# Ternary FFN: biases summed in the matrix products, silu read from its bank, value and product in one pass

## The chip, the cores and the metric

The kernel runs on one core of a Trainium2 chip. The metric is the device time of one execution in microseconds (us), the median of several runs. It is one program of 2.2 ms: four layers, each with a cross attention and a feed-forward network (FFN). The change touches the last FFN alone, which takes the last 130 us.

## What is computed

The activations x are 16 x 128 tokens of 256 features. The last step is `x = x + ffn(layernorm(x))`, with a ternary FFN of 1024 hidden features:

```python
def bit_linear(x, w, b):
    gamma_x = jnp.clip(jnp.max(jnp.abs(x), axis=-1, keepdims=True), 1e-05, None)
    scale_x = 127.0 / gamma_x
    x_dq = jnp.clip(jnp.round(x * scale_x), -128.0, 127.0) / scale_x
    gamma_w = jnp.clip(jnp.mean(jnp.abs(w)), 1e-05, None)
    w_dq = jnp.clip(jnp.round(w / gamma_w), -1.0, 1.0) * gamma_w
    return jnp.einsum('bsd,hd->bsh', x_dq, w_dq) + b
gate = jax.nn.silu(bit_linear(x, gate_w, gate_b))
val = bit_linear(x, val_w, val_b)
return bit_linear(gate * val, out_w, out_b)
```

The kernel multiplies whole numbers held in bf16 (rounded rows by weights of -1, 0 and 1). The sum then has to be multiplied by the row's step (`x_step`, the largest absolute value over 127) and by the weights' mean, and the bias added.

## The kernel before, in words

The 2048 tokens are 16 tiles of 128 rows (`B`), in four groups of four (`GROUP`). `k` is a tile's place in its group. Each engine has its own instruction list, written out in order in `ternary_ffn` (L3369); semaphores (`Signal`) tie the lists together, and `behind(engine, signal, n)` waits for the n-th event, if there is one. Nothing is planned by a program: the order is that of the loops.

TensorE (L3427 to L3469): `up(n, ...)` multiplies tile n by the gate weights into two banks of 512 columns (`gates`), and again by the value weights into two more (`vals`), each bank as two products of 128 rows deep, bf16, 512 columns. For every n its queue holds up(n+1) for the gates, up(n+1) for the values, for k = 2 `turn_rows` (the next group's rounded rows turned), then `turn_product(n)` (eight turns of 128x128, bf16) and `go_down(n)` (eight products of 256 columns into one bank `down`).

VectorE (L3517 to L3581): `halves` reads a bank, multiplies it by the row's scale and adds the bias, for half a tile at a time: gates to `pre`, values to `val` (L3531). `measure(n)` multiplies `val` by silu of `pre` (`prod`, L3547), takes the largest absolute value (L3549), and makes the step and its inverse (L3551, L3552). `finish(n)` adds the downward product to x (L3560). In between stand, for the next group, `norm.scales` and `spread_scales` at k = 0 and `norm.round` at k = 1.

ScalarE (L3471 to L3515): `silu(n)` (L3477, halves), `round_product(n)` (L3481 scales and lifts `prod`, L3484 rounds it to bf16) and `move(n)` (L3489 copies the turned product out of its bank). In iteration n the order is move(n-1), the normalizing of four rows (L2047, at k = 0), their lifting (L2070, at k = 1) or the copy of the turned rows `move_rows` (L3493, at k = 2), round_product(n), silu(n+1).

GpSimd adds the output bias to x (L3425) and takes the root for the norm. SP's queue loads two biases at the start of the stage and stores each tile of the output.

The banks are freed as follows: a gates half once L3531 has read it into `pre`, a values half once L3531 has read it into `val`; `up` waits for that with `behind(pe, read, 2 * (n - 1) + h)`:

```python
for n in range(B):
    if n + 1 < B:
        up(n + 1, gates, w.g, pre_made, gated)
        up(n + 1, vals, w.v, val_made, valued)
    if n % GROUP == 2 and n // GROUP < LASTG:
        turn_rows(n // GROUP + 1)
    turn_product(n)
    go_down(n)
```

The helper `project` (L296) of the first attention, the windowed attention and the mixture-of-experts lines L1861 and L1871 are not touched; the prediction takes durations from them. In `project` two products with f32 operands of 512 columns are issued:

```python
for c in range(HC):
    last = pe.matmul(proj[m % 2][:, :], lhs[:, c, :], weight[:, c, :], start=(c == 0), stop=(c == HC - 1))
```

L1861 copies a bank of 256 columns, L1871 does so with a scale per partition (`moe_share`); L783 is an activation of 512 columns read from a bank.

Of the kernel before, what the change touches and what calls it, by code (L numbers as in the profile page):

```python
# [14 lines left out]
P = 128  # L15
# [911 lines left out]
GROUP = 4  # L927
# [2441 lines left out]
def ternary_ffn(nc, mem, out, stored, norm):  # L3369
# [6 lines left out]
    with ctx:  # L3376
# [11 lines left out]
        pre, gate, val, prod, shifted = (sb(x, [P, F]) for x in ("pre", "gate", "val", "prod", "shifted"))  # L3388
# [18 lines left out]
        pre_made, val_made, silued, multiplied = signal("pre"), signal("val"), signal("silued"), signal("multiplied")  # L3407
# [8 lines left out]
        with nc.Block() as block:  # L3416
# [11 lines left out]
            def _(pe):  # L3428
                def up(n, out_banks, weight, read, done):
                    pe.wait_ge(rows_moved.sem, rows_moved.at(n // GROUP))  # L3430
                    for h in range(2):
                        behind(pe, read, 2 * (n - 1) + h)
                        for c in range(HC):
                            last = pe.matmul(out_banks[h][:, :], mem.xnt16[:, c, n * P:(n + 1) * P], weight[:, c, h * HALF:(h + 1) * HALF], start=(c == 0), stop=(c == HC - 1))  # L3434
                        last.then_inc(done.sem, 1)
# [24 lines left out]
                up(0, gates, w.g, pre_made, gated)  # L3460
                up(0, vals, w.v, val_made, valued)
                for n in range(B):
                    if n + 1 < B:
                        up(n + 1, gates, w.g, pre_made, gated)
                        up(n + 1, vals, w.v, val_made, valued)
# [6 lines left out]
            def _(act):  # L3472
                def silu(n):
                    behind(act, multiplied, n - 1)
                    for h in range(2):
                        act.wait_ge(pre_made.sem, pre_made.at(2 * n + h))
                        act.activation(gate[:, h * HALF:(h + 1) * HALF], pre[:, h * HALF:(h + 1) * HALF], ACT.Silu).then_inc(silued.sem, 1)  # L3477
# [40 lines left out]
            def _(dve):  # L3518
# [6 lines left out]
                def halves(n, target, banks, scale, bias, made, done, read):  # L3525
                    dve.wait_ge(spread.sem, spread.at(2 * (n // GROUP) + 1))
                    for h in range(2):
                        cols = slice(h * HALF, (h + 1) * HALF)
                        dve.wait_ge(made.sem, made.at(2 * n + h))
                        behind(dve, *read(n, h))  # L3530
                        dve.scalar_tensor_tensor(target[:, cols], banks[h][:, :], scale[:, n:n + 1], bias[:, cols], ALU.mult, ALU.add).then_inc(done.sem, 1)  # L3531

                def before_silu(n):
# [390 lines left out]
```

## Time and profile before

| | us |
|---|---|
| median of 3 runs | 2207.52 |
| lowest, highest | 2202.86, 2207.97 |
| the profiled execution | 2204.45 |
| its span, first to last instruction | 2202.7 |
| TensorE busy in the span | 1928.3 (88%) |
| VectorE busy | 1348.5 (61%) |
| ScalarE busy | 1065.7 (48%) |
| GpSimd busy | 717.3 (33%) |

Of the span's 40 slices of 55 us the last two and a half hold the ternary FFN. In the page's rows of engines PE is TensorE's matrix products, PEld its weight loads, DVE VectorE, ACT ScalarE, POOL GpSimd. PEclk is the granted TensorE clock, 1.00 being 2.4 GHz and 0.50 being 1.2 GHz. A row of the timeline has its start and its length in us; where several instructions are merged, "x4" is their number, and the length runs from the first one's start to the last one's end. The bracket at its end is the idle time of the engine ahead of it, with what ended it.

### The profile page before, as it was taken

The page shows a single profiled execution, that of the slowest core. Times are in us where ns is not written, and L with a number is a line of the kernel's source. Part 1 is how long each engine was busy: PE and PEld are TensorE (multiplying, and loading weights), DVE is VectorE, ACT ScalarE, POOL GpSimd, SP SyncE. Part 2 cuts the span into 40 slices and gives each one's busy share as a digit, 9 for nine tenths or more (in the row PEclk, how much of TensorE's full clock was granted, in tenths as well). Part 3 has the DMA queues.
Part 4 walks back from the last instruction along what each step waited for, and adds up shares of the span by engine and source line. Part 5 has one row for each costly group of instructions (what it writes and reads, how often), then busy time and mean ns, then how long its engine had stood idle before and what let it go on. Part 6 is the DMA issues. An engine that isn't in the chain of part 4 may idle for free. (4 is left out here: it accounts for less than half of the span.)

```text
span 2202.7 us, 42217 instructions
## 1 busy us (share of the span) xinstructions
PE 1928.3 (88%) x11925; PEld 1297.9 (59%) x11926; DVE 1348.5 (61%) x3440; ACT 1065.7 (48%) x2793; POOL 717.3 (33%) x691
## 2 busy tenths in 40 slices
PE   7999999998999899979899989979967889888655
PEld 4666666665656566645676667635534557776433
DVE  6556556565777344446443434469969447777687
ACT  5545444553333222112344434357769437677575
POOL 3323333331000004443455556523200026666310
PEclk9999999999999889869999999989979989999787
DMA  9980000000000001143677777600010111111100
GB/s 310 279 223 0 0 0 0 0 1 1 0 0 0 1 1 61 61 162 104 146 160 173 163 164 127 125 1 2 1 60 1 65 36 34 30 40 31 31 17 22
DMA packets 145576, 145.11 MB, mean 66 GB/s; under 512 B 49376, under 2 KB 133568, under 8 KB 145344
## 3 DMA queue, kind: packets, MB, share of 16 engines
q1 hardware_dynamic: 122432, 113.81, 18.2%
q0 software_dynamic: 23040, 30.01, 7.9%
q8 instruction: 53, 0.87, 0.2%
q14 instruction: 51, 0.42, 0.1%
HBM read 137.12 MB, written 66.44 MB: 92 GB/s over the span
## 5 line engine op out<-in xcount | busy, mean ns | idle before, releaser
L1686 POOL DMA_INDIRECT expert_sums<-moe_rows_in,moe_to x128 | 197.9, 1546 | 158.0 <-DMA expert_sums<-moe_rows_in,moe_to 85.9
L1759 PE MATMUL moe_gate<-moe_places,moe_xt 128*128 x512 | 175.5, 465 | 3.1 <-issue 1.9
L1949 DVE COPY moe_ht_e<-moe_turned 128x256 f32<-128x256 f32 x128 | 54.3, 424 | 194.1 <-PE moe_turned L1767 194.1
L619 ACT ACTIVATE ga_prob<-ga_score,ga_neg_max 128x128 f32<-128x128 f32 x256 | 99.5, 390 | 145.7 <-DVE ga_neg_max L493 145.7
L240 POOL TENSOR_TENSOR ga_q_inv<-ga_q_sum,half 128x4 f32<-128x4 f32 x64 | 64.4, 1007 | 304.3 <-DVE ga_q_sum L476 304.3
L3017 POOL TENSOR_TENSOR wa_low<-wa_low,wa_top 128x512 f32<-128x512 f32 x128 | 133.0, 1039 | 89.8 <-DVE wa_top L3221 89.0
L2039 POOL TENSOR_TENSOR ln_rstd<-ln_var,half 128x4 f32<-128x4 f32 (+1 forms) x16 | 21.8, 1361 | 351.9 <-DVE ln_var L2035 351.8
L1153 POOL DMA_INDIRECT slot_x<-early x96 | 93.9, 979 | 112.0 <-DVE early L1144 73.3
L375 PE MATMUL ga_summed<-ga_wo,ga_out_t 128*128 128x256 f32 x512 | 122.5, 383 | 0.7 <-ACT ga_out_t L627 0.7
L375 PEld LDWEIGHTS ga_summed<-ga_wo,ga_out_t 128*128 128x128 f32 x512 | 98.1, 192 | 40.6 <-issue 29.2
L3218 DVE SCALAR_TENSOR_TENSOR wa_low<-wa_score,early 128x512 f32<-128x512 f32 x128 | 87.7, 685 | 55.0 <-PE wa_score L3057 52.5
L299 PE MATMUL ga_proj<-early,ga_xt 128*128 128x512 f32 x252 | 118.6, 593 | 0.0
L1759 PEld LDWEIGHTS moe_gate<-moe_places,moe_xt 128*128 128x128 f32 x512 | 90.7, 189 | 46.6 <-issue 11.5
L489 DVE SCALAR_TENSOR_TENSOR ga_score<-ga_scored,ga_q_inv,ga_mask 128x128 f32<-128x128 f32 x256 | 72.2, 344 | 68.1 <-PE ga_scored L347 51.4
L3155 ACT ACTIVATE wa_probs<-wa_low 128x512 f32<-128x512 f32 x128 | 80.6, 630 | 66.9 <-POOL wa_low L3017 65.9
L3221 DVE TENSOR_REDUCE wa_top<-wa_low 128x4 f32<-128x512 f32 x128 | 87.8, 686 | 4.4
L3057 PE MATMUL wa_score<-wa_keys,wa_qd 32*128 32x128 f32 x1024 | 78.4, 293 | 13.3 <-POOL wa_qd L3011 7.2
L3066 PE MATMUL wa_turned<-ident,wa_probs 128*128 128x128 f32 x512 | 86.4, 294 | 3.6 <-ACT wa_probs L3155 3.0
L1866 ACT ACTIVATE moe_act_e<-moe_gate 128x176 f32<-128x176 f32 x128 | 40.6, 317 | 99.5 <-PE moe_gate L1759 99.5
L506 DVE COPY ga_prob_t<-ga_turned_p 128x256 f32<-128x256 f32 x128 | 48.2, 418 | 65.2 <-PE ga_turned_p L355 65.0
L3057 PEld LDWEIGHTS wa_score<-wa_keys,wa_qd 32*128 32x128 f32 x1024 | 66.1, 195 | 27.5 <-issue 25.3
L3161 ACT ACTIVATE wa_pt<-wa_turned 128x512 f32<-128x512 f32 x128 | 74.4, 581 | 13.1 <-PE wa_turned L3066 13.0
(482 smaller groups left out, 4952.0 us busy)
## 6 DMA issues: line engine op xcount, KB each, us to landing
moe_places<-in_L_ffn_packed SPq DMA_DIRECT2D x128, 608.0 KB
slot_x<-zeros SPq DMA_DIRECT2D x24, 1076.0 KB, 16.1
moe_rows_in<-slot_x SPq DMA_DIRECT2D x128, 134.5 KB, 2.7
wa_v<-v_ctx SPq DMA_DIRECT2D x16, 180.0 KB, 3.1
early<-in_L_xattn_Wq SPq DMA_DIRECT2D x5, 512.0 KB, 7.8
x<-in_x SPq DMA_DIRECT2D x4, 512.0 KB, 9.2
ga_wo<-in_L_xattn_Wo SPq DMA_DIRECT2D x1, 2048.0 KB, 14.0
expert_sums<-zeros SPq DMA_DIRECT2D x2, 1024.0 KB, 8.2
```

Source lines behind the costliest of these rows:

```text
L299: last = pe.matmul(proj[m % 2][:, :], lhs[:, c, :], weight[:, c, :], start=(c == 0), stop=(c == HC - 1))
L375: last = pe.matmul(summed[:, 0:H], out_t[:, h, :], w.wo[:, h, :], start=(h == 0), stop=(h == NH - 1))
L619: last = act.activation(prob[:, n % 2, part], score[:, n % 2, part], ACT.Exp, bias=neg_max[:, n % 2, h:h + 1], accum_out=total[:, n % 2, h ...
L1153: pool.indirect_dma_start(out=self.mem.slot_x, out_offset=bass.IndirectOffsetOnAxis(ap=self.slot_to[:, t, k:k + 1], axis=0), in_=self.mem. ...
L1686: pool.indirect_dma_start(out=mem.sums[j % SUMS], out_offset=bass.IndirectOffsetOnAxis(ap=to[:, j:j + 1], axis=0), in_=y[:, j, :], in_offs ...
L1759: last = pe.matmul(both[j % 2][:, 0:2 * FE], xt[:, j % 2, c, :], packed[:, place, c * 2 * FE:(c + 1) * 2 * FE].rearrange("p a n -> p (a n) ...
L3017: pool.tensor_tensor(unit, unit, top[:, k % LOWS, :].unsqueeze(2).to_broadcast([P, QUAD, P]), ALU.subtract).then_inc(lowered.sem, 1)
L3057: last = pe.matmul(score[BANK[r]][:, x * P:(x + 1) * P], qd[rows, j % 2, QUAD * u + x, :], keys[rows, j % 2, QUAD * u + x, :], start=True, ...
L3066: last = pe.transpose(turned[k % 2][:, x * P:(x + 1) * P], probs[:, k % 2, x, :], mem.ident[:, :])
L3155: act.activation(probs[:, k % 2, :, :], low[:, k % LOWS, :, :], ACT.Exp).then_inc(exped.sem, 1)
L3218: dve.scalar_tensor_tensor(unit.rearrange("p x n -> p (x n)"), score[BANK[k % QUAD]][:, :], WD ** -0.5, w.table[:, k, :, :].rearrange("p x ...
L3221: dve.tensor_reduce(top[:, k % LOWS, :], unit, AX.X, ALU.max).then_inc(topped.sem, 1)
```

## The change

The bias is summed by TensorE. The bank holds whole numbers that are later multiplied by step and mean, so the bias must go in divided by both: once at the start `bias_over_mean` divides the two bias tiles (128x1024, f32, in place) by the weights' means, and `spread_inverse(n)` makes, for each tile, a 128x128 f32 diagonal of the rows' inverse steps (two buffers). `up` gets a third product per half: diagonal by bias, 512 columns, both operands f32, in the same accumulation. The gates' bank is then read by ScalarE's silu, with the scale as its operand, and `pre` goes; the values' bank is read by the product pass, half by half, and `val` goes. So a gates half is free after silu, a values half after the product.

```diff
--- before.py
+++ after.py
@@ -3385,7 +3385,8 @@
 
         w = mem.tf
         scale_g, scale_v = sb("scale_g", [P, B]), sb("scale_v", [P, B])
-        pre, gate, val, prod, shifted = (sb(x, [P, F]) for x in ("pre", "gate", "val", "prod", "shifted"))
+        gate, prod, shifted = (sb(x, [P, F]) for x in ("gate", "prod", "shifted"))
+        diagonal, per_mean = sb("diagonal", [P, 2, P]), sb("per_mean", [P, 2])
         rounded = sb("rounded", [P, F], BF16)
         ht = sb("ht", [P, FC, P], BF16)
         up_by, down_by = sb("up_by", [P, 1]), sb("down_by", [P, 1])
@@ -3404,7 +3405,8 @@
         spread = signal("spread")
         biased = signal("biased")
         gated, valued = signal("gated"), signal("valued")
-        pre_made, val_made, silued, multiplied = signal("pre"), signal("val"), signal("silued"), signal("multiplied")
+        diagonals, per_means, biases = signal("diagonals"), signal("per_means"), signal("biases")
+        silued, multiplied = signal("silued"), signal("multiplied")
         chain, per_made = signal("chain"), signal("per")
         lifted, rounded_s = signal("lifted"), signal("rounded")
         turn, moved, downed, added = signal("turn"), signal("moved"), signal("downed"), signal("added")
@@ -3426,13 +3428,16 @@
 
             @block.tensor
             def _(pe):
-                def up(n, out_banks, weight, read, done):
+                def up(n, out_banks, weight, bias, j, read, done):
                     pe.wait_ge(rows_moved.sem, rows_moved.at(n // GROUP))
                     for h in range(2):
                         behind(pe, read, 2 * (n - 1) + h)
                         for c in range(HC):
-                            last = pe.matmul(out_banks[h][:, :], mem.xnt16[:, c, n * P:(n + 1) * P], weight[:, c, h * HALF:(h + 1) * HALF], start=(c == 0), stop=(c == HC - 1))
-                        last.then_inc(done.sem, 1)
+                            pe.matmul(out_banks[h][:, :], mem.xnt16[:, c, n * P:(n + 1) * P], weight[:, c, h * HALF:(h + 1) * HALF], start=(c == 0), stop=False)
+                        if h == 0:
+                            pe.wait_ge(diagonals.sem, diagonals.at(n))
+                            pe.wait_ge(biases.sem, biases.at(j))
+                        pe.matmul(out_banks[h][:, :], diagonal[:, n % 2, :], bias[:, h * HALF:(h + 1) * HALF], start=False, stop=True).then_inc(done.sem, 1)
 
                 def turn_rows(g):
                     pe.wait_ge(norm.rounded.sem, norm.rounded.at(g * GROUP + GROUP - 1))
@@ -3457,12 +3462,12 @@
                     last.then_inc(downed.sem, 1)
 
                 turn_rows(0)
-                up(0, gates, w.g, pre_made, gated)
-                up(0, vals, w.v, val_made, valued)
+                up(0, gates, w.g, w.bg, 0, silued, gated)
+                up(0, vals, w.v, w.bv, 1, multiplied, valued)
                 for n in range(B):
                     if n + 1 < B:
-                        up(n + 1, gates, w.g, pre_made, gated)
-                        up(n + 1, vals, w.v, val_made, valued)
+                        up(n + 1, gates, w.g, w.bg, 0, silued, gated)
+                        up(n + 1, vals, w.v, w.bv, 1, multiplied, valued)
                     if n % GROUP == 2 and n // GROUP < LASTG:
                         turn_rows(n // GROUP + 1)
                     turn_product(n)
@@ -3471,10 +3476,11 @@
             @block.scalar
             def _(act):
                 def silu(n):
-                    behind(act, multiplied, n - 1)
+                    act.wait_ge(spread.sem, spread.at(2 * (n // GROUP)))
                     for h in range(2):
-                        act.wait_ge(pre_made.sem, pre_made.at(2 * n + h))
-                        act.activation(gate[:, h * HALF:(h + 1) * HALF], pre[:, h * HALF:(h + 1) * HALF], ACT.Silu).then_inc(silued.sem, 1)
+                        behind(act, multiplied, 2 * (n - 1) + h)
+                        act.wait_ge(gated.sem, gated.at(2 * n + h))
+                        act.activation(gate[:, h * HALF:(h + 1) * HALF], gates[h][:, :], ACT.Silu, scale=scale_g[:, n:n + 1]).then_inc(silued.sem, 1)
 
                 def round_product(n):
                     act.wait_ge(per_made.sem, per_made.at(n))
@@ -3522,17 +3528,15 @@
                     for scale, mean_of in ((scale_g, w.mean_g), (scale_v, w.mean_v)):
                         dve.tensor_scalar(scale[:, cols], mem.x_step[:, cols], mean_of[:, 0:1], None, ALU.mult).then_inc(spread.sem, 1)
 
-                def halves(n, target, banks, scale, bias, made, done, read):
-                    dve.wait_ge(spread.sem, spread.at(2 * (n // GROUP) + 1))
-                    for h in range(2):
-                        cols = slice(h * HALF, (h + 1) * HALF)
-                        dve.wait_ge(made.sem, made.at(2 * n + h))
-                        behind(dve, *read(n, h))
-                        dve.scalar_tensor_tensor(target[:, cols], banks[h][:, :], scale[:, n:n + 1], bias[:, cols], ALU.mult, ALU.add).then_inc(done.sem, 1)
-
-                def before_silu(n):
-                    halves(n, pre, gates, scale_g, w.bg, gated, pre_made, lambda n, h: (silued, 2 * (n - 1) + h))
-                    halves(n, val, vals, scale_v, w.bv, valued, val_made, lambda n, h: (multiplied, n - 1))
+                def spread_inverse(n):
+                    if n % GROUP == 0:
+                        dve.wait_ge(norm.scaled.sem, norm.scaled.at(n // GROUP))
+                    behind(dve, valued, 2 * (n - 2) + 1)
+                    dve.tensor_scalar(diagonal[:, n % 2, :], mem.ident[:, :], norm.scale[:, n:n + 1], None, ALU.mult).then_inc(diagonals.sem, 1)
+
+                def bias_over_mean(j, bias):
+                    dve.wait_ge(per_means.sem, per_means.at(j))
+                    dve.tensor_scalar(bias[:, :], bias[:, :], per_mean[:, j:j + 1], None, ALU.mult).then_inc(biases.sem, 1)
 
                 def measure(n):
                     j = slice(n % 2, n % 2 + 1)
@@ -3541,11 +3545,14 @@
                         ins.then_inc(chain.sem, 1)
                         dve.wait_ge(chain.sem, chain.at(2 * n + k))
 
-                    dve.wait_ge(silued.sem, silued.at(2 * n + 1))
-                    dve.wait_ge(val_made.sem, val_made.at(2 * n + 1))
+                    dve.wait_ge(spread.sem, spread.at(2 * (n // GROUP) + 1))
                     behind(dve, lifted, n - 1)
-                    dve.tensor_tensor(prod[:, :], val[:, :], gate[:, :], ALU.mult).then_inc(multiplied.sem, 1)
-                    dve.wait_ge(multiplied.sem, multiplied.at(n))
+                    for h in range(2):
+                        dve.wait_ge(valued.sem, valued.at(2 * n + h))
+                        dve.wait_ge(silued.sem, silued.at(2 * n + h))
+                        dve.scalar_tensor_tensor(prod[:, h * HALF:(h + 1) * HALF], vals[h][:, :], scale_v[:, n:n + 1], gate[:, h * HALF:(h + 1) * HALF],
+                                                 ALU.mult, ALU.mult).then_inc(multiplied.sem, 1)
+                    dve.wait_ge(multiplied.sem, multiplied.at(2 * n + 1))
                     step(0, dve.tensor_reduce(far[:, j], prod[:, :], AX.X, ALU.max, apply_absolute_value=True))
                     behind(dve, added, n - 2)
                     step(1, dve.tensor_scalar(size[:, j], far[:, j], 1e-5, 1.0 / 127.0, ALU.max, ALU.mult))
@@ -3560,12 +3567,18 @@
                     dve.scalar_tensor_tensor(row, down[:, 0:H], scale_o[:, n % 2:n % 2 + 1], row, ALU.mult, ALU.add).then_inc(added.sem, 1)
 
                 spread_scales(0)
+                spread_inverse(0)
+                for j, mean_of in enumerate((w.mean_g, w.mean_v)):
+                    dve.reciprocal(per_mean[:, j:j + 1], mean_of[:, 0:1]).then_inc(per_means.sem, 1)
+                bias_over_mean(0, w.bg)
                 norm.variance(dve, LASTG * GROUP, B)
                 norm.shifts(dve, 1, LASTG * GROUP, B)
                 dve.wait_ge(mem.tf_loaded.sem, 16 * 3)
-                before_silu(0)
+                bias_over_mean(1, w.bv)
                 for n in range(B):
                     g, k = divmod(n, GROUP)
+                    if n + 1 < B:
+                        spread_inverse(n + 1)
                     measure(n)
                     if k == 0 and g < LASTG:
                         norm.scales(dve, g + 1)
@@ -3574,8 +3587,6 @@
                         if g >= 2:
                             dve.wait_ge(turned_rows.sem, turned_rows.at(g - 1))
                         norm.round(dve, g + 1)
-                    if n + 1 < B:
-                        before_silu(n + 1)
                     if n >= 1:
                         finish(n - 1)
                 finish(B - 1)
```

## Rows read from the trace of the kernel before

**Rows 1.** Windows of the ternary FFN: us, busy us (count) by engine, PEclk, DMA share, GB/s.

```profile
2105.00:2135.00 30.00, 18.46 (x106) 10.10 (x104) 26.22 (x50) 22.59 (x29) 2.77 (x4) 0.78 0.05 18
```

**Rows 2.** Chain that ended last, near its end: start us, us, what.

```profile
2184.43 1.23 DVE tf_far L3549
...
2186.07 1.25 ACT tf_shifted L3481
...
2187.41 0.04 ACT tf_rounded L3484
...
2188.46 1.14 ACT tf_gate L3477 x2
...
2189.63 1.24 DVE tf_prod L3547
```

**Rows 3.** Timeline of the ternary FFN: start us, us, engine, line, what [idle before].

```profile
2095.37 1.05 PE L3456 MATMUL tf_down<-tf_o,tf_ht 128*128 128x256 bf16 x8 [1.33 <-ACT tf_ht L3489]
...
2096.25 1.03 PE L3434 MATMUL tf_gates<-tf_g,tf_xnt 128*128 128x512 bf16 x4
...
2097.59 1.40 DVE L3531 SCALAR_TENSOR_TENSOR tf_pre<-tf_gates,tf_scale_g,early 128x512 f32<-128x512 f32 x2
...
2098.62 1.02 ACT L3493 ACTIVATE tf_xnt<-tf_turned_in 128x1024 bf16<-128x1024 bf16 x1 [3.31 <-PE tf_turned_in L3442]
...
2102.07 0.62 PE L3449 MATMUL tf_turned<-ident,tf_rounded 128*128 128x128 bf16 x8 [3.48 <-ACT tf_rounded L3484]
...
2102.96 1.00 ACT L3489 ACTIVATE tf_ht<-tf_turned 128x1024 bf16<-128x1024 bf16 x1
...
2104.02 1.89 PE L3456 MATMUL tf_down<-tf_o,tf_ht 128*128 128x256 bf16 x8 [1.32 <-ACT tf_ht L3489]
...
2105.70 1.56 PE L3434 MATMUL tf_gates<-tf_g,tf_xnt 128*128 128x512 bf16 x4
...
2110.32 2.07 ACT L2047 ACTIVATE tf_rows_of<-x,ln_shift,ln_rstd 128x256 f32<-128x256 f32 x4
...
2110.47 1.05 PE L3456 MATMUL tf_down<-tf_o,tf_ht 128*128 128x256 bf16 x8 [1.33 <-ACT tf_ht L3489]
...
2125.19 1.05 PE L3456 MATMUL tf_down<-tf_o,tf_ht 128*128 128x256 bf16 x8 [1.12 <-ACT tf_ht L3489]
...
2134.05 1.89 PE L3456 MATMUL tf_down<-tf_o,tf_ht 128*128 128x256 bf16 x8 [1.12 <-ACT tf_ht L3489]
...
2140.29 1.05 PE L3456 MATMUL tf_down<-tf_o,tf_ht 128*128 128x256 bf16 x8 [1.33 <-ACT tf_ht L3489]
```

**Rows 4.** Groups by line and shape: busy us, mean ns of one, idle before.

```profile
L1178 DVE TENSOR_SCALAR early<-ident,early 128x128 f32<-128x128 f32 x1 | 0.3, 289 | 0.0
...
L783 ACT ACTIVATE sf_act_g<-sf_gate 128x512 f32<-128x512 f32 x32 | 19.1, 596 | 93.6 <-PE sf_up L743 93.6
...
L1861 ACT ACTIVATE moe_xt<-moe_up 128x256 f32<-128x256 f32 x128 | 49.2, 384 | 48.6 <-PE moe_up L1748 38.0
...
L1871 ACT ACTIVATE moe_rows_in<-moe_pairs,moe_share 128x256 f32<-128x256 f32 x64 | 30.3, 473 | 31.3 <-PE moe_pairs L1774 31.3
```

**Rows 5.** Timeline of TensorE in the first attention, and windows of two attentions.

```profile
51.91 1.88 PE L299 MATMUL ga_proj<-early,ga_xt 128*128 128x512 f32 x4
...
44.00:64.00 20.00, 19.66 (x106) 14.78 (x105) 13.97 (x42) 13.91 (x59) 7.44 (x9) 1.00 0.79 217
...
1840.00:1860.00 20.00, 17.29 (x299) 13.72 (x298) 16.09 (x31) 14.06 (x26) 12.37 (x13) 1.00 0.15 30
```

**Rows 6.** Timeline around the start of the ternary FFN.

```profile
2057.39 1.14 DVE L2065 TENSOR_SCALAR early<-early,ln_scale 128x256 f32<-128x256 f32 x4
...
2075.47 1.89 PE L3434 MATMUL tf_gates<-tf_g,tf_xnt 128*128 128x512 bf16 x4 [1.18 <-ACT tf_xnt L3493]
...
2080.02 1.03 PE L3434 MATMUL tf_vals<-tf_v,tf_xnt 128*128 128x512 bf16 x4
```

**Rows 7.** Timeline at the end of the span.

```profile
2199.23 0.48 DVE L3560 SCALAR_TENSOR_TENSOR x<-tf_down,tf_scale_o,x 128x256 f32<-128x256 f32 x1 [6.24 <-PE tf_down L3456]
```

## The prediction, made before the change was run

> **What bounds the kernel now.** I read the windows first, then the chain of waits, then the timeline of one tile, then the costs by shape. The windows say where the stage stands [rows 1]: in the ternary FFN VectorE is busy 26.2 of 30 us, ScalarE 22.6, TensorE 18.5 at a mean granted clock of 0.78. So VectorE looks like the bound, and the change unloads it. The chain corrects this [rows 2]: near the end one loop closes in about 6.45 us: product 1.24, maximum 1.23, step and inverse 0.41 up to the start of the scaling, scaling 1.25 and 0.09 of waits, rounding 1.05 until silu can follow it, silu 1.14, and some 0.06 of waits. It crosses VectorE and ScalarE, and TensorE is not in it. In the timeline the reader should look for what is queued on TensorE: down(n-1), gates and values of n+1, turn of the product n, in that fixed order. One group of four tiles takes 29.8 us (down at 2110.47 to down at 2140.29), and in each group ScalarE stands 3.31 us in front of the row copy L3493, because TensorE turns the rows only behind the up products [rows 3].
>
> A measurement of this kernel can tell about 0.3% (7 us) from no change.
>
> **Part 1, removed from VectorE.** Four L3531 passes (two in 1.40 us, so 2.80) and one L3547 (1.24) go; two passes of L3531's kind, bank times scalar times SBUF tile, come back at 1.40; the new diagonal is 128x128 in f32, 0.29 us by L1178's row, less beside others. Net 4.04 - 1.69 = 2.3 us per tile less VectorE [rows 2 to 4]. That is 37 us over 16 tiles, but only a stretch that ends on VectorE gives any of it back.
>
> **Part 2, silu from the bank.** From a bank 128x512 takes 0.60 us (L783), and a scale per partition costs 0.473 - 0.384 = 0.09 more (L1871 against L1861): 0.69. The pair, 1.14 now, goes to about 1.28 (0.69 and 0.60 behind it): +0.15 on ScalarE [rows 2, 4]. The product can now start on half 0 when silu of half 0 is done. The old loop becomes: silu 0.69, two product passes with the second from 1.37 to 2.11, maximum until 3.37, step and inverse until 3.75, scaling and rounding until the next silu at 6.15. So without TensorE the loop would be 6.15 instead of 6.45.
>
> **Part 3, the bias in the accumulator.** Four matrix products of 128x512 per tile are added, with both operands f32. What they cost stands elsewhere in this trace: the project helper issues two f32 products of 128x512, and the trace has four records in 1.88 us at clock 1.00, that is four times 0.427 and 0.17 of fill [rows 5]. So one f32 product is two records, 0.853 us; the bf16 one takes 0.213 (four in 1.03, with the same fill) [rows 6]. Per tile: 4 x 0.853 = 3.41 us more on TensorE at full clock, 6.8 at half clock. Bounds: not under 0.213 each (bf16's row, if the form did not matter), not over 1.71 (half clock throughout). I take 0.853, from the same shape and type.
>
> TensorE's queue is in order and closes its own loop: from down to the up products 0.88 (2095.37 to 2096.25); up 4 x 0.213 x 2 = 1.71, with the biases 5.12; turn 0.62; semaphore 0.05; ScalarE's copy L3489 1.00; semaphore 0.06; next down. **7.75 us** per tile. That is above 6.15 and above today's 6.45, so TensorE becomes the bound. New waits, and who queues there: the gates of n+1 wait for silu(n), the values for product(n); counted from the end of up(n), product(n) ends 0.75 later (the second half's pass behind its values), maximum, step, inverse, scaling and rounding take the way to 4.9, silu(n+1) ends at 6.2 and product(n+1) at 8.5, while the gates of n+2 come up at 10.35 (7.75 + 0.62 + 1.11 + 0.88) and their values at 12.9. Both waits are met 4 us early, so they cost nothing; with that cover gone, TensorE and everything in its queue would stand for what silu or product is late. The waits on the diagonals and biases stand ahead of the first bias product of each half; VectorE makes the diagonal of n+1 ahead of measure(n), one tile early: nothing. No DMA is added or moved, SP's queue is as before. GpSimd's biases of x and its root stay; only the first root comes later (below).
>
> The normalizing rows on ScalarE (2.07 us, twice in a group) [rows 3] fall into its idle time: its own work there is 1.28 + 1.00 + 2.07 + 2.39 = 6.7, under 7.75. So tiles k = 0, 1 and 3 of a group take 7.75; today k = 0 and 1 take 14.72 together (2110.47 to 2125.19) and k = 3 takes 6.24 (2134.05 to 2140.29) [rows 3].
>
> **The tile k = 2** is the expensive one. Its way is down, up products, turn of the rows, row copy L3493, scaling and rounding, silu, copy of the turned product, down: 8.65 us in the first group (2095.37 to 2104.02), 8.86 in the second (2125.19 to 2134.05) [rows 3]. All of the up products lie on it, so it becomes 12.2 to 12.4 with 3.41 and 0.15 added; I take 12.3.
>
> **The clock.** In the trace TensorE drops to half after this very gap: idle 3.48 us, turn, idle again, then down in 1.89 instead of 1.05 and the gates behind it in 1.56 [rows 3]. The changed kernel keeps a gap of about 3.4 us there. Down and most of the gates, 3 us of work, run at half clock in that row, so 1.5 us are lost; the drop may last some gates longer, 2.1 at most by my estimate if all of the gates are in it. It now lies on the path, as up does. I take 1.7 per group. Elsewhere TensorE has 6.65 us of work in 7.75, and the windowed attention, busy 17.29 of 20 us, runs at 1.00 [rows 5]. The Trainium skill, page "TensorE: Matmul & The Clock Gate", section "What's actually happening", says that activity releases the throttle and idleness brings it back; read so, denser work might keep the full clock through this gap too, and then the terms for it fall away. By that rule the trace agrees that gaps precede the drops; it does not show TensorE this busy beside such a gap. This is rival A.
>
> **Start.** VectorE does the bias pass of 1024 columns ahead of variance. Its price: 0.29 for 128 columns, and four passes of 256 in 1.14 us give up to 0.27 per 256; so 0.5 to 1.2, I take 1.0 [rows 4, 6]. The gates start at 2075.47 as now, the bias is ready near 2075.1; root and shift end near 2077.2, the bias of the values near 2078.2, all ahead of TensorE. It is at half clock at first (four products in 1.89) and back at full before 2080.02 (1.03); I take 2079.6. So gates are done at 2080.1, values at 2082.65, product(0) at 2083.45 [rows 6]. Maximum, step and inverse take it to 2085.05, scaling and rounding to 2087.4, silu(1) to 2088.65, the copy to 2089.65: down(0) comes at about 2089.7.
>
> **Sum.** Down(0) 2089.7; +7.75; +12.3; +7.75 + 1.7 gives down(3) at 2119.2. Two groups of 7.75 x 3 + 12.3 + 1.7 = 37.25: down(11) at 2193.7. Down(13) two loops later, 2209.2. Product(15) ends 6.0 + 0.75 behind it: 2215.95. From the end of product(15) (2189.63 + 1.24) to the end of the span today 2202.7 - 2190.87 = 11.83 us pass, the last addition at 2199.23 in them, and that tail is untouched [rows 2, 7]. End 2227.8: **+25 us** on the span of 2202.7. The profiled execution's own time of 2204.45 becomes 2229.5; it lies 3.1 us under the median of the three runs, 2207.52, so the median should come near 2232 by the one reference and 2229.5 by the other. I predict 2231, between them.
>
> **Rivals.**
> A. As above but the clock holds at full behind the row copy: 3 x 1.7 less, +20, 2226. For it: TensorE does more between the gaps. Against: the 3.48 us gap shown is followed by half clock, and so is its like in the next group, down again 1.89 at 2134.05 [rows 3].
> B. Half clock reaches further, for the small gap of 1.1 us in every tile: some 2 us more in each of half a dozen tiles, +37, 2243. The trace has a gap of 1.33 us in front of a down at full clock (1.05) [rows 3], so I hold it unlikely.
> C. The other side, faster: the accumulation hides the bias at bf16's price. TensorE's loop is then 0.88 + 2.56 + 0.62 + 1.11 = 5.2 and the loop of 6.15 decides, the point being a bias product under about 0.45 us (7.75 - 4 x 0.4 = 6.15). Plain tiles gain 0.3; with the pressure off VectorE the tiles with normalizing gain up to 1; k = 2 still gets longer by about 1.0. Together up to 1 per group and 1 to 4 over the rest: 2195 to 2204, under 0.3% for the most part, the low end only if the clock holds too. Against it stand the two records per f32 product [rows 5].
> D. VectorE is the bound after all, as its busy share says: 16 x 2.3 = 37 us less, 2170. Against: in rows 2 it waits for ScalarE's silu, and TensorE's 7.75 is above either loop.
> E. The edit does not do what it says, the f32 pair is skipped or merged: same as C at its upper end, no change.
>
> **Chances.** Forecast 0.66, A 0.16, B 0.10, C 0.05 (0.03 of it faster), D 0.01, E 0.02. Slower by over 0.3% is 0.92, within 0.04, faster 0.04. The range takes in A and goes 7 us under it, for the start (1 us), for a k = 2 tile at its lower value and for the 5 us by which the runs differ; above it goes to the near part of B: 2219 to 2241. It leaves out C, D, E and half of B, 0.13, and tails.
>
> **What the new profile would show.** Right: four bias products per tile as eight records of 0.427 us spacing; TensorE busy over 85% in the stage; plain tiles 7.75 apart, the k = 2 tile near 12.3; VectorE idle in front of the product with the values named as releaser; down in 1.89 behind the row copy. Wrong: bias records with bf16's spacing, ScalarE's silu instead of TensorE's values in front of the product, or plain tiles near 6.2, each of which would put the result at or under today's time.

## The result and the profile after

The changed kernel takes 2231.91 us (median of four runs, 2226.65 to 2245.17) against 2207.74 for the kernel before (four runs, 2202.86 to 2213.69): a ratio of 1.0118, with a 95% interval of 1.0082 to 1.0155. It is slower by 24 us by the medians and by 26 by the ratio; 2231 was predicted. That agreement has to be read with a margin: the profiled execution has a span of 2235.2 us against 2202.7, which is 32.5 more, and only part of that belongs to the change. Its first gate product starts 6.7 us later (2082.16 against 2075.47), behind stages that are the same code in both kernels. The part from there to the end of the span, "the stage" below, is what the change touches: 2202.7 - 2075.47 = 127.23 us before, 2235.2 - 2082.16 = 153.04 after, 25.8 us more. The prediction's own times (2227.8 - 2075.47) make it 152.3.

The windows of the changed kernel, with the columns of [rows 1]:

```profile
2105.00:2135.00 30.00, 23.17 (x108) 12.40 (x107) 13.55 (x32) 17.79 (x23) 2.79 (x4) 0.89 0.04 13
2165.00:2200.00 35.00, 28.17 (x127) 14.57 (x125) 15.90 (x37) 20.64 (x26) 1.94 (x3) 0.90 0.05 16
```

VectorE's 26.2 of 30 us [rows 1] are down to 13.6, so the unloading worked as built. Over the whole stage its work falls less, from 103.2 to 70.6 us, 2.03 per tile; the rest of the fall in the window is that the tiles are longer. TensorE is up from 18.5 to 23.2 and its clock from 0.78 to 0.89, and the stage is longer all the same. The chain of waits says why. Its columns are start us, us, what. The four pieces of f32 products (L3440) take 3.4 of each 7.8 us:

```profile
2096.48 1.05 PE tf_down L3461 x8
2097.96 0.86 PE tf_gates L3440 x2
2099.25 0.86 PE tf_gates L3440 x2
2100.54 0.86 PE tf_vals L3440 x2
2101.83 0.86 PE tf_vals L3440 x2
2103.17 1.03 ACT tf_ht L3495
2104.25 1.05 PE tf_down L3461 x8
```

Nothing of VectorE is in this stretch, and of ScalarE only the copy L3495. This is TensorE's own loop: 2096.48 to 2104.25 is 7.77 us. The chain of [rows 2], product, maximum, scaling, rounding, silu, is gone from it.

Groups by line and shape in the stage, after (busy us, mean ns, idle before and what ended it):

```profile
L3440 PE MATMUL tf_gates<-early,tf_diagonal 128*128 128x512 f32 x64 | 35.9, 645 | 0.0
L3440 PE MATMUL tf_vals<-tf_bv,tf_diagonal 128*128 128x512 f32 x64 | 32.7, 592 | 0.0
L3553 DVE SCALAR_TENSOR_TENSOR tf_prod<-tf_vals,tf_scale_v,tf_gate 128x512 f32<-128x512 f32 x32 | 23.6, 750 | 65.7 <-PE tf_vals L3440 38.0 <-ACT tf_gate L3483 27.7
```

The price is in the counts: 64 f32 products are issued, one for each of two biases, two halves and 16 tiles. Each of the two groups has 64 records for 32 products, so two per product. VectorE's product pass stood 65.7 us idle, 38.0 of them for TensorE's values.

The timeline of TensorE over the k = 2 tile, after, and then the row copy on ScalarE:

```profile
2108.15 1.02 PE L3440 MATMUL tf_vals<-tf_bv,tf_diagonal 128*128 128x512 f32 x2
...
2110.30 0.61 PE L3447 MATMUL tf_turned_in<-ident,tf_out_of 128*128 128x128 bf16 x8
2114.39 1.03 PE L3454 MATMUL tf_turned<-ident,tf_rounded 128*128 128x128 bf16 x8 [3.48 <-ACT tf_rounded L3490]
2116.54 1.89 PE L3461 MATMUL tf_down<-tf_o,tf_ht 128*128 128x256 bf16 x8 [1.12 <-ACT tf_ht L3495]
2118.22 1.06 PE L3436 MATMUL tf_gates<-tf_g,tf_xnt 128*128 128x512 bf16 x2
2119.08 1.65 PE L3440 MATMUL tf_gates<-early,tf_diagonal 128*128 128x512 f32 x2
...
2126.16 1.05 PE L3461 MATMUL tf_down<-tf_o,tf_ht 128*128 128x256 bf16 x8 [1.12 <-ACT tf_ht L3495]
```

```profile
2110.94 1.02 ACT L3499 ACTIVATE tf_xnt<-tf_turned_in 128x1024 bf16<-128x1024 bf16 x1 [6.75 <-PE tf_turned_in L3447]
```

This answers [rows 3]. ScalarE stands 6.75 us in front of the row copy instead of 3.31; TensorE's gap of 3.48 us is there again; behind it the turns (1.03) and down (1.89) run at half clock, then the gates, and full clock is back within the first f32 pair (1.65, where a pair takes 1.02 at full clock). The tile k = 2 takes 2116.54 - 2104.25 = 12.29 us, the one behind it 9.62, the next 7.77.

### The profile page after: what moved, and what is told of

It is laid out like the page before. It is cut to its first block and busy times, and to the rows that moved or that the text cites. A ratio compares the mean times of both kernels' runs of the same rounds, so it can differ in the third digit from the quotient of the medians.

```text
span 2235.2 us, 42466 instructions
## 1 busy us (share of the span) xinstructions
PE 1980.5 (89%) x12053; PEld 1325.0 (59%) x12054; DVE 1316.8 (59%) x3412; ACT 1069.5 (48%) x2793; POOL 717.1 (32%) x691
## 5 line engine op out<-in xcount | busy, mean ns | idle before, releaser
L1759 PEld LDWEIGHTS moe_gate<-moe_places,moe_xt 128*128 128x128 f32 x512 | 91.4, 191 | 47.1 <-issue 12.3
L3057 PEld LDWEIGHTS wa_score<-wa_keys,wa_qd 32*128 32x128 f32 x1024 | 67.3, 199 | 27.7 <-issue 25.5
## 6 DMA issues: line engine op xcount, KB each, us to landing
ga_wo<-in_L_xattn_Wo SPq DMA_DIRECT2D x1, 2048.0 KB, 14.2
```

Of the source, the lines that this page charges most:

```text
L1759: last = pe.matmul(both[j % 2][:, 0:2 * FE], xt[:, j % 2, c, :], packed[:, place, c * 2 * FE:(c + 1) * 2 * FE].rearrange("p a n -> p (a n) ...
L3057: last = pe.matmul(score[BANK[r]][:, x * P:(x + 1) * P], qd[rows, j % 2, QUAD * u + x, :], keys[rows, j % 2, QUAD * u + x, :], start=True, ...
```

## The experiments

The ratio is that of each kernel against the kernel before on the same chip; e1 to e4 ran on one chip, e5 to e8 on a second, e9 and e10 on a third, so whole times of different groups are not compared. In these traces the first gate product starts anywhere from 2075 to 2109 us, up to 34 us apart and up to 16.5 on one chip, in code that no kernel here changes, so the stage is the sharper measure. It comes from one trace per kernel; how far it repeats is known only from e3 and e10, the same kernel on two chips: 117.3 and 117.0. Where the trace lacks the record of the first gate product (the idle time ahead of the first one shown is 1.58 us instead of 1.18), 0.4 us are added; those are marked with a star.

| kernel | bias products | rows turned | stage, us | ratio (95% interval) |
|---|---|---|---|---|
| before | none, biases on VectorE | behind up | 127.2 | 1 |
| the change | f32 | behind up | 153.0 | 1.0118 (1.0082 to 1.0155) |
| e1_fp16 | fp16 | behind up | 127.1 | 1.001 (0.9991 to 1.0028) |
| e2_early | f32 | ahead of up | 135.7 | 1.0056 (1.0036 to 1.0075) |
| e3_fp16_early | fp16 | ahead of up | 117.3 | 0.9948 (0.9927 to 0.9969) |
| e4_before_early | none, on VectorE | ahead of up | 121.7 | 0.9993 (0.9972 to 1.0015) |
| e5_double | f32, twice | behind up | 208.1* | not known, one run |
| e6_warm | f32, one gap filled | behind up | 150.4* | 1.0112 (1.0082 to 1.0143) |
| e7_half | f32, gates only | behind up | 130.6* | 1.0034 (1.0005 to 1.0062) |
| e8_nobias | left out | behind up | 120.5* | 0.9974 (0.9952 to 0.9995) |
| e9_warm2 | f32, both gaps filled | behind up | 147.6* | 1.008 (1.0045 to 1.0114) |
| e10_fp16_early2 | as e3 | ahead of up | 117.0* | 0.9927 (0.9897 to 0.9958) |

### Is it the price of the f32 products?

e1_fp16 writes the diagonal and the divided biases as 16-bit floats and changes nothing else:

```diff
-        diagonal, per_mean = sb("diagonal", [P, 2, P]), sb("per_mean", [P, 2])
+        diagonal, per_mean = sb("diagonal", [P, 2, P], F16), sb("per_mean", [P, 2])
+        bias_g, bias_v = sb("bias_g", [P, F], F16), sb("bias_v", [P, F], F16)
...
-                up(0, gates, w.g, w.bg, 0, silued, gated)
+                up(0, gates, w.g, bias_g, 0, silued, gated)
...
-                    dve.tensor_scalar(bias[:, :], bias[:, :], per_mean[:, j:j + 1], None, ALU.mult).then_inc(biases.sem, 1)
+                    dve.tensor_scalar(out[:, :], bias[:, :], per_mean[:, j:j + 1], None, ALU.mult).then_inc(biases.sem, 1)
```

> The diagonal and the two bias tiles are written as 16-bit floats (fp16), so each bias product is of the bf16 kind; everything else is the changed kernel. Theory P (the price of the f32 products, 0.853 us each, makes TensorE the bound): one record per bias product at 0.21 us spacing, TensorE's loop falls from 7.77 to about 5.2 us, the loop through silu, product and rounding (6.15) decides in plain tiles, the k = 2 tile near 9.6 to 9.8; the stage from its first gate product to the end of the span falls from 153 to about 122 to 127 us, the whole to 2195 to 2208. Rival S (it is the structure: silu and the product now hold the banks and the chain): the stage stays above 145 us.

Measured: the stage falls from 153.0 to 127.1, the upper edge of what was expected, and the kernel is back at the time of the one before. Same rows, same banks, same waits: so the structure (rival S) is not what costs. An fp16 bias product (f16 in the rows) is one record, and the next product starts 0.22 us behind it. Timeline of TensorE, e1:

```profile
2116.76 1.05 PE L3463 MATMUL tf_down<-tf_o,tf_ht 128*128 128x256 bf16 x8 [1.12 <-ACT tf_ht L3497]
...
2118.07 0.38 PE L3442 MATMUL tf_gates<-tf_bias_g,tf_diagonal 128*128 128x512 f16 x1
2118.29 0.59 PE L3438 MATMUL tf_gates<-tf_g,tf_xnt 128*128 128x512 bf16 x2
...
2126.39 1.89 PE L3463 MATMUL tf_down<-tf_o,tf_ht 128*128 128x256 bf16 x8 [1.44 <-ACT tf_ht L3497]
...
2134.15 1.05 PE L3463 MATMUL tf_down<-tf_o,tf_ht 128*128 128x256 bf16 x8 [1.12 <-ACT tf_ht L3497]
...
2138.48 0.62 PE L3456 MATMUL tf_turned<-ident,tf_rounded 128*128 128x128 bf16 x8 [0.69 <-ACT tf_rounded L3492]
2140.54 1.05 PE L3463 MATMUL tf_down<-tf_o,tf_ht 128*128 128x256 bf16 x8 [1.44 <-ACT tf_ht L3497]
```

The k = 2 tile (2116.76 to 2126.39) takes 9.63 instead of 12.29, a tile with normalizing rows (2134.15 to 2140.54) 6.39, where 6.15 was expected. What keeps the stage from the lower edge is the clock: tile 1 takes 8.09 and the first two k = 3 tiles 7.76 and 8.03, with most of their up products at half clock. Now TensorE waits 0.69 us for ScalarE's rounding in front of the turns, which it did not in the f32 version.

e5_double goes the other way and issues the f32 bias product twice, so that the biases count double:

```diff
+                        pe.matmul(out_banks[h][:, :], diagonal[:, n % 2, :], bias[:, h * HALF:(h + 1) * HALF], start=False, stop=False)
                         pe.matmul(out_banks[h][:, :], diagonal[:, n % 2, :], bias[:, h * HALF:(h + 1) * HALF], start=False, stop=True).then_inc(done.sem, 1)
```

> The f32 bias product is issued twice in each half (the bias counts double in the output). Theory P: every tile is on TensorE's loop, so each tile gets 4 x 0.853 = 3.41 us more: plain tiles 11.18, the k = 2 tile 15.7, the stage 153 + 16 x 3.41 = 207.6 us. Rival S (the structure limits): TensorE has slack and the stage grows by under 30 us.

```profile
2111.03 1.05 PE L3462 MATMUL tf_down<-tf_o,tf_ht 128*128 128x256 bf16 x8 [1.12 <-ACT tf_ht L3496]
...
2122.24 1.05 PE L3462 MATMUL tf_down<-tf_o,tf_ht 128*128 128x256 bf16 x8 [1.12 <-ACT tf_ht L3496]
...
2137.96 1.89 PE L3462 MATMUL tf_down<-tf_o,tf_ht 128*128 128x256 bf16 x8 [1.12 <-ACT tf_ht L3496]
```

In this timeline of TensorE a plain tile takes 11.21 us, 3.44 more than 7.77, and the k = 2 tile 15.72, 3.43 more than 12.29. The stage grows by 55.0 us, 16 times 3.44. Every 0.853 us added to TensorE is paid in full: in the changed kernel it has no slack.

e7_half leaves the bias of the values out of the computation, e8_nobias both biases. The edit of e7, whose bf16 products then end the accumulation where no bias product follows:

```diff
-                        pe.matmul(out_banks[h][:, :], diagonal[:, n % 2, :], bias[:, h * HALF:(h + 1) * HALF], start=False, stop=True).then_inc(done.sem, 1)
+                        if j == 0:
...
+                            last = pe.matmul(out_banks[h][:, :], diagonal[:, n % 2, :], bias[:, h * HALF:(h + 1) * HALF], start=False, stop=True)
+                        last.then_inc(done.sem, 1)
```

> The f32 bias product is issued for the gates alone; the values' bias is left out of the computation. Theory P: TensorE's loop is 7.77 - 1.71 = 6.06, just under the loop through silu and product as the fp16 version showed it (6.27 in the last group), so plain tiles in the last group take 6.3 and those with normalizing rows 6.4; k = 2 takes 12.29 - 1.71 = 10.6, k = 3 some 8; a group 31.4, the stage about 132 us. If the cost per product were all that counts, without a second loop, plain tiles would be 6.06.

```profile
2192.86 1.05 PE L3463 MATMUL tf_down<-tf_o,tf_ht 128*128 128x256 bf16 x8 [1.12 <-ACT tf_ht L3497]
...
2198.98 1.05 PE L3463 MATMUL tf_down<-tf_o,tf_ht 128*128 128x256 bf16 x8 [1.18 <-ACT tf_ht L3497]
...
2205.25 1.05 PE L3463 MATMUL tf_down<-tf_o,tf_ht 128*128 128x256 bf16 x8 [1.33 <-ACT tf_ht L3497]
```

The last group of e7 runs at 6.12 and 6.27 us per tile (2192.86, 2198.98, 2205.25). In the groups before it, tiles with normalizing rows take 6.40 and k = 2 10.48 to 10.57. From down(1) to down(5) are 31.7, and the stage is 130.6 where about 132 was expected. TensorE's own loop would be 6.06. The 6.40 lies clear of it, so there the loop through ScalarE and VectorE decides. In the last group the two are too close to tell: its tiles take 6.05, 6.12, 6.27 and 6.13.

> No bias product at all (both biases are left out); the diagonals are still made. Theory P: nothing is gained over the fp16 version in plain tiles (6.3 to 6.4, set by ScalarE and VectorE), and 0.85 us in each k = 2 tile (8.8): the stage about 124.5 us against its 127.1. Rival S: as in the fp16 version, over 145.

Timeline of TensorE, e8:

```profile
2177.61 1.05 PE L3458 MATMUL tf_down<-tf_o,tf_ht 128*128 128x256 bf16 x8 [1.37 <-ACT tf_ht L3492]
...
2183.89 1.05 PE L3458 MATMUL tf_down<-tf_o,tf_ht 128*128 128x256 bf16 x8 [1.45 <-ACT tf_ht L3492]
```

Measured: plain tiles 6.27 and 6.28, those with normalizing rows mostly 6.39 as in e1, k = 2 8.77 and 8.85, the stage 120.5 where 124.5 was expected. The rule for plain tiles held, and 6.27 is the loop without TensorE. The miss of 4 us lies mostly in tiles that run at half clock: there TensorE's loop is the longer one again, and a bias product left out is worth 0.43 us instead of 0.21. Tile 1 takes 6.39 in e8 and 8.09 in e1, the first two k = 3 tiles 7.18 and 6.19 against 7.76 and 8.03. With e1, e5, e7 and e8 the curve is known for tiles at full clock: flat up to some 6.2 us of TensorE loop, and one to one above.

### Is it the row turns behind the up products?

e2_early moves one statement in TensorE's list:

```diff
                 for n in range(B):
+                    if n % GROUP == 2 and n // GROUP < LASTG:
+                        turn_rows(n // GROUP + 1)
                     if n + 1 < B:
                         up(n + 1, gates, w.g, w.bg, 0, silued, gated)
                         up(n + 1, vals, w.v, w.bv, 1, multiplied, valued)
-                    if n % GROUP == 2 and n // GROUP < LASTG:
-                        turn_rows(n // GROUP + 1)
                     turn_product(n)
```

> The changed kernel with f32 products, but at k = 2 TensorE turns the next group's rows ahead of the up products instead of behind them. Theory P: the k = 2 tile no longer has all up products ahead of the row copy; it falls from 12.29 to about 8.2 us (7.77 and the turns), the gap of 3.48 us goes and the half clock behind it too, so the next tile falls from 9.62 to about 7.8; together 3 x 5.9 = 18 us less than the changed kernel, about 2214, and the stage 135. Rival: the row copy is not what holds the tile, then under 5 us are gained.

```profile
2119.24 1.05 PE L3461 MATMUL tf_down<-tf_o,tf_ht 128*128 128x256 bf16 x8 [1.12 <-ACT tf_ht L3495]
2120.12 0.61 PE L3447 MATMUL tf_turned_in<-ident,tf_out_of 128*128 128x128 bf16 x8
...
2127.45 1.05 PE L3461 MATMUL tf_down<-tf_o,tf_ht 128*128 128x256 bf16 x8 [1.12 <-ACT tf_ht L3495]
```

The k = 2 tile is 2127.45 - 2119.24 = 8.21 us, no gap is left but the 1.12 us in front of down, and down runs at 1.05. The stage falls by 17.3 us: the f32 products are dearest where the whole of up stands ahead of something that ScalarE waits for.

e4_before_early is the same move in the kernel before.

> The kernel before, with only the rows turned ahead of the up products at k = 2. ScalarE's wait of 3.31 us in front of the row copy falls to about 1.3, so some 2 us per group are gained, 6 in all: about 2201, the stage 121. If VectorE's 26 of 30 us are the true bound of that kernel, it gains nothing.

```profile
2113.88 1.02 ACT L3493 ACTIVATE tf_xnt<-tf_turned_in 128x1024 bf16<-128x1024 bf16 x1 [1.58 <-PE tf_turned_in L3442]
```

ScalarE's wait for the row turns falls from 3.31 to 1.58 us, the stage from 127.2 to 121.7 as expected. The times of the whole kernel show less, 0.9993 with an interval that holds 1: 5.5 us are a quarter of a per cent, which these runs cannot tell. With e2 this says what the order has to do with the change: the order alone is worth 5.5 us without bias products. With the rows turned early in both kernels, the f32 biases cost 14.0 us (121.7 to 135.7) instead of 25.8. So 11.8 of the 25.8 us hang on the order.

e3_fp16_early puts fp16 and the early row turns together.

> Both of the former: fp16 bias products and the rows turned early. Theory P: ScalarE's own work decides at k = 0 and 1 (6.75), k = 2 near 7.3, k = 3 near 6.2, a group 27 instead of 29.8 us before the change; the stage about 115 to 118 us instead of 127, the whole about 2196, 0.5% faster than before. Rival S: not faster than before.

```profile
2128.07 1.05 PE L3463 MATMUL tf_down<-tf_o,tf_ht 128*128 128x256 bf16 x8 [1.12 <-ACT tf_ht L3497]
...
2135.12 1.89 PE L3463 MATMUL tf_down<-tf_o,tf_ht 128*128 128x256 bf16 x8 [1.45 <-ACT tf_ht L3497]
...
2146.14 0.62 PE L3456 MATMUL tf_turned<-ident,tf_rounded 128*128 128x128 bf16 x8 [0.69 <-ACT tf_rounded L3492]
2148.21 1.70 PE L3463 MATMUL tf_down<-tf_o,tf_ht 128*128 128x256 bf16 x8 [1.45 <-ACT tf_ht L3497]
...
2155.09 1.05 PE L3463 MATMUL tf_down<-tf_o,tf_ht 128*128 128x256 bf16 x8 [1.12 <-ACT tf_ht L3497]
...
2201.86 1.05 PE L3463 MATMUL tf_down<-tf_o,tf_ht 128*128 128x256 bf16 x8 [1.45 <-ACT tf_ht L3497]
...
2208.13 1.05 PE L3463 MATMUL tf_down<-tf_o,tf_ht 128*128 128x256 bf16 x8 [1.45 <-ACT tf_ht L3497]
```

A group (2128.07 to 2155.09) takes 27.0 us, 27 expected; the k = 2 tile 7.05, plain tiles of the last group 6.27. The tiles k = 0 and 1 take 6.40 and 6.88, not 6.75 each. The stage is 117.3 us, 10 less than before the change and 36 less than after it. Of the 10 us, 5.5 are the order's (e4) and 4.4 belong to the change with fp16 biases (121.7 to 117.3). The ratio of 0.9948 is clear of 1 and of the change's 1.0118. It was run again:

> The version with fp16 bias products and the rows turned early once more, on whatever chip comes: the earlier stages differ by up to 20 us from run to run, so its gain of 0.5% over the kernel before is to be seen a second time. By the stages (117.3 against 127.2 us) it should be 10 us, a ratio of 0.995.

Measured: 0.9927 (0.9897 to 0.9958), the stage 117.0. This version beats both kernels. Its biases carry the rounding of fp16 twice, in the inverse step and in the bias over the mean.

### Is half clock behind the gap the gap's doing?

e6_warm gives TensorE something to do in the 3.48 us:

```diff
+        idle = bank("idle")
...
                         turn_rows(n // GROUP + 1)
+                        for i in range(14):
+                            pe.matmul(idle[:, :], mem.xnt16[:, 0, n * P:(n + 1) * P], w.g[:, 0, 0:HALF], start=True, stop=True)
```

> The changed kernel with 14 idle bf16 products of 512 columns (3.0 us at full clock, into a bank of their own that nobody reads) behind the turns of the rows at k = 2, where TensorE stands 3.48 us. Clock theory: the gap is filled, so the down behind it takes 1.05 instead of 1.89 us and its tile 7.8 instead of 9.6; three times 1.85 = 5.5 us less, the stage 147.5. Rival: the fall has another cause; down stays at 1.89 and the stage at 153.

```profile
2107.13 2.97 PE L3475 MATMUL tf_idle<-tf_g,tf_xnt 128*128 128x512 bf16 x13
2110.56 0.62 PE L3455 MATMUL tf_turned<-ident,tf_rounded 128*128 128x128 bf16 x8 [0.46 <-ACT tf_rounded L3493]
2112.63 1.53 PE L3462 MATMUL tf_down<-tf_o,tf_ht 128*128 128x256 bf16 x8 [1.45 <-ACT tf_ht L3498]
```

A half miss. The turns run at full clock now, but the clock falls inside the down behind them: 1.53 us here, 1.19 in the second group, 1.05 in the third, where no fall comes. The tile behind takes 9.45, about as long as 9.62, in the first group and 7.77 in the third. The stage falls to 150.4. Two gaps are left, 0.46 and 1.45 us, so e9_warm2 fills the second as well:

```diff
                     turn_product(n)
+                    if n % GROUP == 2 and n // GROUP < LASTG:
+                        for i in range(5):
+                            pe.matmul(idle[:, :], mem.xnt16[:, 0, n * P:(n + 1) * P], w.g[:, 0, 0:HALF], start=True, stop=True)
                     go_down(n)
```

> The changed kernel with both gaps of the k = 2 tile filled: 14 idle bf16 products behind the turns of the rows, and 5 more (1.07 us) between the turns of the product and down. With the first gap alone filled, the clock still fell in two of three groups, late, inside down or right behind it. Clock theory: with both filled it stays at full in all three, every down but the last takes 1.05, every k = 3 tile 7.8, the stage 147.5 us. Rival: what is left of the fall does not come from the gaps; one or more of the three downs is still slow and the stage at 150.

```profile
2137.58 0.62 PE L3455 MATMUL tf_turned<-ident,tf_rounded 128*128 128x128 bf16 x8 [0.46 <-ACT tf_rounded L3496]
2138.03 1.24 PE L3479 MATMUL tf_idle<-tf_g,tf_xnt 128*128 128x512 bf16 x5
2139.64 1.05 PE L3462 MATMUL tf_down<-tf_o,tf_ht 128*128 128x256 bf16 x8 [0.37 <-ACT tf_ht L3501]
```

Every down but the last takes 1.05 us, in all three groups; each k = 3 tile takes 7.77; the stage is 147.6. The fall belongs to the gaps, both of them, and costs 5.4 us in this kernel. The products whose result nobody reads lengthen nothing, as TensorE stood still there: the k = 2 tile takes 12.20.

## Why the prediction was right, point by point

- **f32 products.** 0.853 us each and two records per product were taken from the projections of the first attention [rows 5]. The trace after has 64 records for 32 products, and e5 measures 3.44 per tile for four, 0.86 each. Rival C, bf16's price, is excluded.
- **TensorE's loop.** 7.75 predicted, 7.77 measured in every tile with k = 0 or 1 and in the last group up to down(14). The move of the bound from the VectorE and ScalarE loop to TensorE was right.
- **The k = 2 tile.** 12.3 predicted, 12.29, 12.28 and 12.29 measured.
- **The clock.** 1.7 us per group predicted, 9.62, 9.67 and 9.69 less 7.77 is 1.85, 1.90 and 1.92 measured. Three times that is 5.7 instead of 5.1. Rival A (full clock through the gap) did not come: TensorE's denser work did not hold it. By the Trainium skill, page "TensorE: Matmul & The Clock Gate", section "What's actually happening", activity releases the throttle and idleness brings it back. The traces agree on both sides: with the gap half clock in three of three groups, with both gaps filled in none. Rival B (half clock in further tiles, for the gap of 1.1 us) did not come either.
- **The other loop.** 6.15 without TensorE was predicted, 6.27 is what e3 and e8 show: some 0.1 us too low, off the path in this kernel. ScalarE's own 6.7 us in tiles with normalizing rows was too high: e1, e3 and e7 do such tiles in 6.40. Rival C's sum, 2195 to 2204, was too low: e1 is that case, and it gives the time before, a ratio of 1.001. The gain in tiles k = 0 and 1 and the loss at k = 2 are there, but the sum had no term for k = 3 tiles at half clock, 7.76 and 8.03 us instead of 6.24 to 6.45.
- **Start.** Down(0) was to come 14.2 us behind the first gate product (2089.7 - 2075.47) and comes 14.32 behind it (2096.48 - 2082.16). VectorE's bias pass, put at 1.0 us, took 0.75 and 1.32.
- **End.** From the end of product(15) to the end of the span 11.83 us were taken over from before; it is 2235.2 - 2223.72 = 11.48. Product(15) was to end 6.75 behind down(13) and ends 7.01 behind it (2223.72 - 2216.71), so the two misses nearly cancel.
- **What was off.** "TensorE busy over 85% in the stage" was wrong: 23.17 of 30 us are 77% and 28.17 of 35 are 80%, since the k = 2 tile holds a gap of 3.48 and one of 1.12 us. And of VectorE's idle time in front of the product 27.7 us, in four waits of up to 8.9, were ended by silu, not by the values. The prediction had named that as a sign of being wrong; the long ones are the k = 2 tiles, where silu stands behind the row copy in ScalarE's list, and say nothing against TensorE as the bound. The columns are us, times, the longest:

```profile
DVE tf_prod L3553 <- PE tf_vals L3440: 38.0, 24, 4.3
DVE tf_prod L3553 <- ACT tf_gate L3483: 27.7, 4, 8.9
```

- **How exact it was.** By the stage, 25.8 us against 25, and the mechanism is the one that was forecast. The agreement of the medians to 1 us is luck: the four runs lie between 2226.65 and 2245.17, and the stages ahead of the FFN move by more than 1 us from run to run.
- **Rival D** (VectorE is the bound, 37 us gained) is what the busy shares alone would have said; VectorE's fell by half and nothing was gained.

## What to carry to other kernels

Moving work from a busy engine to one with a lower busy share pays only if the receiver's own queue, closed to a loop with its waits, stays under the loop that bounds now. Here it came to 7.77 against 6.45 us, and that could be worked out from rows of the same trace. Before an f32 operand goes to TensorE for a small correction, look up what the same shape costs elsewhere in the profile, count its records, and ask whether 16 bits will do: the type alone was worth 26 us of 153. And look at what stands behind the block that grows: the order of one statement, the row turns ahead of or behind up, decided over 17 us of the changed kernel.

## What the runs showed of the hardware that was not expected

Short pauses alone can bring the clock down. Filling the 3.48 us gap down to 0.46 was not enough: the clock fell in two of three groups, later than before, as long as 1.45 us in front of down stayed open, although gaps of 1.12 us in every other tile never brought it down. In e3 there is no long gap at all: from down(1) to down(14) TensorE never stands longer than 1.45 us, yet five of the downs take 1.57 to 1.89 us, as the one at 2148.21 does behind gaps of 0.69 and 1.45 us. In e1 nearly the same pair of gaps (0.69 and 1.44) stands in front of the down at 2140.54, which takes 1.05. In e2, where each tile has only the 1.12 us left, the granted clock is 1.00 from 2110 to 2225. So filling a long gap is not enough where the work around it leaves TensorE other pauses. What exactly decides is left open, and e3 would still gain by holding the clock: behind the down at 2148.21 the next tile takes 6.88 us, where e1 has 6.40 for the same tile at full clock.

VectorE's bias pass of 1024 columns takes 0.75 us alone and 1.32 beside GpSimd's additions, and the diagonal of 128 columns 0.28 and 0.74. Timeline of the start, after:

```profile
2080.24 0.28 DVE L3535 TENSOR_SCALAR tf_diagonal<-ident,ln_scale 128x128 f32<-128x128 f32 x1
...
2080.62 0.75 DVE L3539 TENSOR_SCALAR early<-early,tf_per_mean 128x1024 f32<-128x1024 f32 x1
...
2083.52 1.32 DVE L3539 TENSOR_SCALAR tf_bv<-tf_bv,tf_per_mean 128x1024 f32<-128x1024 f32 x1 [0.17 <-DMA tf_bo<-in_L_ffn_out_b]
2083.57 3.22 POOL L3427 TENSOR_TENSOR x<-x,tf_bo 128x256 f32<-128x256 f32 x4 [0.40 <-DMA tf_bo<-in_L_ffn_out_b]
...
2084.76 0.74 DVE L3535 TENSOR_SCALAR tf_diagonal<-ident,ln_scale 128x128 f32<-128x128 f32 x1
```

The Trainium skill, page "SBUF — State Buffer", section "SBUF: two separate sides", says of the pair of ports which VectorE and GpSimd share that it is an exclusive lock, held for a whole instruction, so that the other one blocks; for VectorE it names instructions in a two-port mode or with two SBUF inputs. The trace fits it in part: 0.57 and 0.46 us more where both engines are at work, less than one of GpSimd's additions (0.7 to 0.9). But the pass at 2083.52 starts ahead of the first addition, so by that rule it should not have waited, no row tells the mode, and no run here was made to separate these. So the cause is not shown. The longer passes cost nothing, as TensorE came to these tiles later.
